# Cross attention in a decoder layer: orders of their own for the second group of heads

## The reference, cut to what matters

```
q = split_heads(x @ Wq)          # x (8, 224, 512), 16 heads of 64
k = split_heads(context @ Wk)    # context (8, 750, 384)
v = split_heads(context @ Wv)
sim = einsum('bhid,bhjd->bhij', q, k) * SCALE
attn = softmax(sim)
out = einsum('bhij,bhjd->bhid', attn, v)
x = layernorm(x + (merge(out) @ Wo + bo))
```

## Time and profile before

| | us |
|---|---|
| median of three runs | 1943.18 |
| the profiled execution, its own time | 1947.31 |
| its span, first to last instruction | 1945.7 |
| step of group one, from Y0 to Y0 | 69.39 |
| step of group two, from Y0 to Y0 | 68.76 |
| steps whose order changes | 8 |

### The profile page before, as it was taken

The page is one execution under the profiler, slowest core; times in us unless marked ns, Lnnn a source line. Parts: engine busy times, 40 slices in busy tenths (PEclk is TensorE's granted clock), DMA queues, the critical chain, the costliest instruction groups (busy, mean ns, idle before and its releaser), DMA issues.

```text
span 1945.7 us, 39197 instructions
## 1 busy us (share of the span) xinstructions
PE 1847.2 (95%) x12618; PEld 1514.6 (78%) x12618; DVE 1471.7 (76%) x3326; ACT 1172.2 (60%) x2568; POOL 999.7 (51%) x1065
## 2 busy tenths in 40 slices
PE   5999998999998999999999999999999999988997
PEld 4777776777776898899899888888888888874443
DVE  5677677788888777777777777877777777777887
ACT  5676776675675466566656666655555555554664
POOL 0343443244343266665675644567677667540554
PEclk9899999999997999999999999999999999999999
DMA  4321323011113414322431432313332331252221
GB/s 127 125 71 61 103 80 105 29 38 47 29 46 108 153 46 139 120 93 96 140 99 62 158 104 60 104 49 92 107 87 64 84 107 44 66 125 72 65 65 60
DMA packets 109571, 166.76 MB, mean 86 GB/s; under 512 B 32488, under 2 KB 67672, under 8 KB 109512
## 3 DMA queue, kind: packets, MB, share of 16 engines
q1 hardware_dynamic: 91016, 129.77, 21.7%
q0 software_dynamic: 14656, 28.92, 5.2%
q10 hardware_dynamic: 3840, 7.34, 1.3%
HBM read 109.25 MB, written 50.46 MB: 82 GB/s over the span
## 4 chain that ended last, share of the span: by engine, by line
PE 56%; DVE 16%; issue 11%; ACT 5%; POOL 5%; DMA 5%; POOLq 0%; SPq 0%; DVEq 0%; ACTq 0%
PE att_ps_P L1477 9%; PE att_ps_P L1489 9%; PE att_ps_T L1523 7%; PE att_ps_O L1537 6%; PE att_ps_SA L1512 5%; PE att_ps_O L1548 4%; PE att_ps_P L1466 4%; PE att_ps_T L451 3%; DVE sa_sums L751 2%; PE att_ps_SB L513 2%; DMA out_dram<-ff_y_out 2%; DVE ca_big L1772 2%; DVE att_ps_O L1904 1%; DMA sa_ff_in<-in_L_ffn_w_gate_dram 1%; PE att_ps_P L468 1%
## 5 line engine op out<-in xcount | busy, mean ns | idle before, releaser
L1345 POOL TENSOR_TENSOR ca_pr<-ca_pr,ca_rec 112x750 f32<-112x750 f32 x256 | 364.2, 1440 | 249.6 <-DVE ca_rec L1767 247.0
L392 POOL TENSOR_TENSOR sa_p_lo<-sa_pr,sa_p_hi 112x448 fp32r<-112x448 f32 x128 | 147.9, 1161 | 330.2 <-ACT sa_p_hi L599 330.2
L1657 ACT ACTIVATE ca_big<-att_ps_T 126x448 fp32r<-126x448 f32 x374 | 204.0, 546 | 137.9 <-PE att_ps_T L1523 134.0
L1772 DVE TENSOR_TENSOR ca_big<-att_ps_T,ca_big 126x448 fp32r<-126x448 f32 x374 | 231.8, 620 | 36.3 <-ACT ca_big L1657 28.4
L1489 PE MATMUL att_ps_P<-ca_w_hi,ca_ct 128*126 128x256 f32 x1152 | 236.8, 290 | 4.7 <-DVE ca_v_st L1755 4.2
L1523 PE MATMUL att_ps_T<-att_ident,ca_pr 112*126 112x112 f32 x1496 | 211.9, 263 | 8.0 <-DVE ca_big L1772 6.2
L1477 PE MATMUL att_ps_P<-ca_ct,ca_w_hi 128*128 128x376 f32 x768 | 201.4, 343 | 0.0
L1523 PEld LDWEIGHTS att_ps_T<-att_ident,ca_pr 112*126 112x126 f32 x1496 | 159.6, 140 | 51.7 <-issue 26.6
L1489 PEld LDWEIGHTS att_ps_P<-ca_w_hi,ca_ct 128*126 128x126 f32 x1152 | 185.5, 187 | 15.8 <-issue 8.5
L1537 PE MATMUL att_ps_O<-ca_big,ca_v_st 126*128 126x448 f32 x756 | 183.6, 378 | 5.8 <-DVE ca_big L1772 3.0
L1489 PE MATMUL att_ps_P<-ca_w_lo,ca_ct 128*126 128x256 f32 x576 | 162.3, 282 | 0.0
(11 more groups left out here) (271 smaller groups left out, 5611.8 us busy)
## 6 DMA issues: line engine op xcount, KB each, us to landing
ct_kept<-ca_ct SPq DMA_DIRECT2D x8, 1134.0 KB, 9.1
ca_ct<-ct_kept POOLq DMA_DIRECT2D x8, 1134.0 KB, 7.1
ct_kept<-ca_ct SPq DMA_DIRECT2D x8, 1116.0 KB, 11.4
ca_ct<-ct_kept POOLq DMA_DIRECT2D x8, 1116.0 KB, 10.9
sa_xin<-in_x_dram SPq DMA_DIRECT2D x16, 448.0 KB, 3.7
xt_kept<-ca_xt SPq DMA_DIRECT2D x8, 896.0 KB, 4.9
ca_xt<-xt_kept POOLq DMA_DIRECT2D x8, 896.0 KB, 4.9
ternary<-ca_stage SPq DMA_DIRECT2D x36, 172.0 KB, 1.9
```

The source lines that it names most:

```text
L392: pool.tensor_tensor(p_lo[:, h % NB, :], pr[:, h % NB, :], f32(p_hi[:, h % NB, :]), ALU.subtract).then_inc(p_split, 1)
L1345: pool.tensor_tensor(w, w, rec[:, h % PB, c:c + 1].to_broadcast([R, S]), ALU.mult).then_inc(norm_done, 1)
L1657: act.activation(weights_view(h, t, False), blocks_view(source.bank, t), ACT.Copy).then_inc(t_hi_done, 1)
L1772: dve.tensor_tensor(weights_view(h, t, True), blocks_view(source.bank, t), f32(weights_view(h, t, False)), ALU.subtract).then_inc(source.d ...
```

## The change

The second group gets orders of its own on PE, ACT and DVE, instead of the common order with XT and CT skipped. The list of projection units that says which bank each uses gets a second form as well. The common orders stay as they were for the first group, the orders of POOL and SP too, and no arithmetic changes. The 66 units of PE, 72 of ACT and 105 of DVE in a step are the same ones as before, moved. At the switch between the groups, the splits of new weights that hung on XT0, XT1, CT00, K30, K31, V11 and V13 hang on T3.0, Q0, K31, V11, V12 and V13.

Below, each "-" order is the one before with XT and CT taken out, as it is carried out in the second group; each "+" order is the new one.

```diff
-    UNITS = """XT0 XT1 CT00 Q0 CT01 CT02 CT10 CT11 V00 V01 V02 Q1 Q2 CT12 K00 K01 K10 K11 K20 K21 V03 Q3 V04 V05 V10 K30 K31
-               V11 V12 V13 V14 V15""".split()
+    UNITS_2 = """Q0 V00 V01 V02 Q1 Q2 K00 K01 K10 Q3 K11 K20 K21 V03 V04 V05 K30 V10 K31 V11 V12 V13 V14 V15""".split()
...
# PE
-  S2.1 T3.0 Q0+ T3.1 O2 T3.2 S3.0 T4.0 O3 T4.1 V00+ V01+ T4.2 S3.1 V02+ T5.0 Q1+ Q2+ T5.1 O4 T5.2 K00+ K01+ T6.0 K10+ T6.1
-  K11+ T6.2 O5 S0.0+ T7.0 K20+ K21+ T7.1 O6 V03+ T7.2 S0.1+ Q3+ O7 T0.0+ V04+ V05+ T0.1+ S1.0+ V10+ T0.2+ Y0 S1.1+ T1.0+ Y1
-  T1.1+ K30+ K31+ O0+ S2.0+ T1.2+ V11+ V12+ T2.0+ V13+ V14+ T2.1+ V15+ O1+ T2.2+
+  S2.1 T3.0 Q0+ T3.1 O2 T3.2 S3.0 T4.0 O3 T4.1 V00+ V01+ T4.2 S3.1 V02+ T5.0 O4 Q1+ T5.1 Q2+ T5.2 K00+ T6.0 K01+ T6.1 O5
+  K10+ T6.2 S0.0+ Q3+ T7.0 K11+ K20+ T7.1 O6 K21+ T7.2 S0.1+ V03+ V04+ T0.0+ O7 V05+ S1.0+ T0.1+ K30+ T0.2+ V10+ Y0 S1.1+
+  T1.0+ Y1 T1.1+ K31+ S2.0+ T1.2+ V11+ O0+ T2.0+ V12+ V13+ T2.1+ V14+ O1+ T2.2+ V15+
# ACT (cut)
-  T3.0 S4.1 Q0+ T3.1 S5.1 O2 T3.2 T4.0 S6.0 O3 T4.1 S7.0 V00+ V01+ T4.2 V02+ S6.1 T5.0 S7.1 ...
+  T3.0 S4.1 T3.1 S5.1 O2 Q0+ T3.2 T4.0 O3 S6.0 T4.1 S7.0 V00+ V01+ T4.2 T5.0 V02+ O4 S6.1 ...
# DVE
-  M4.1 T3.0 M5.1 Q0+ T3.1 R4.1 R5.1 O2 T3.2 M6.0 T4.0 ... M2.0+ M3.0+ V10+ R2.0+ T0.2+ R3.0+ Y0 M2.1+ M3.1+ T1.0+ R2.1+ R3.1+
-  Y1 F0 T1.1+ F1 K30+ F2 O0+ F3 K31+ F4 M4.0+ F5 T1.2+ F6 V11+ F7 M5.0+ F8 V12+ F9 R4.0+ F10 T2.0+ F11 V13+ F12 V14+ F13
-  T2.1+ F14 R5.0+ V15+ O1+ T2.2+
+  M4.1 T3.0 M5.1 R4.1 T3.1 O2 T3.2 R5.1 Q0+ M6.0 T4.0 ... M2.0+ K30+ M3.0+ T0.2+ R2.0+ Y0 V10+ M2.1+ M3.1+ T1.0+
+  Y1 F0 T1.1+ F1 R3.0+ F2 F3 F4 K31+ M4.0+ F5 T1.2+ R2.1+ F6 M5.0+ V11+ T2.0+ F7 V12+ O0+ F8 R3.1+ F9 F10 T2.1+ F11 F12
+  V13+ F13 V14+ R4.0+ F14 T2.2+ R5.0+ O1+ V15+
...
-                       B - 1: {"XT0": [7], "XT1": [8], "CT00": [9], "K30": [10], "K31": [11], "V11": [12], "V13": [13]}}
+                       B - 1: {"T3.0": [7, 8], "Q0": [9], "K31": [10], "V11": [11], "V12": [12], "V13": [13]}}
...
+    def order_for(orders, ahead):
+        return orders[ahead.group if ahead else GROUPS - 1]
...
-                    if ahead and not (ahead.group and name[0:2] in CACHED):
+                    if ahead:
```

More of the change, by code:

```diff
@@ L1019, in banks @@
         return Banks(slots)
[L1021 to L1024, removed]
+    assert sorted(UNITS_2) == sorted(u for u in UNITS_1 if u[0:2] not in ("XT", "CT"))
+    UNITS = [UNITS_1, UNITS_2]
+    plans, front = [banks(units) for units in UNITS], banks(FRONT)
+    last_units = UNITS_1[UNITS_1.index("V10"):]
+    assert sorted(FRONT) == sorted(UNITS_1) and FRONT[-len(last_units):] == last_units
     def batch(b, g, ahead=0):
@@ L1549, in project_out @@
             mm.then_inc(to.filled, 1)
-        ORDER = steps("""XT0+ XT1+ S2.1 T3.0 CT00+ Q0+ T3.1 CT01+ O2 T3.2 CT02+ CT10+ S3.0 T4.0 CT11+ O3 T4.1 V00+ V01+ T4.2 S3.1 V02+
+        ORDERS = [steps("""XT0+ XT1+ S2.1 T3.0 CT00+ Q0+ T3.1 CT01+ O2 T3.2 CT02+ CT10+ S3.0 T4.0 CT11+ O3 T4.1 V00+ V01+ T4.2 S3.1 V02+
                    T5.0 Q1+ Q2+ T5.1 O4 CT12+ T5.2 K00+ K01+ T6.0 K10+ T6.1 K11+ T6.2 O5 S0.0+ T7.0 K20+ K21+ T7.1 O6 V03+ T7.2
                    S0.1+ Q3+ O7 T0.0+ V04+ V05+ T0.1+ S1.0+ V10+ T0.2+ Y0 S1.1+ T1.0+ Y1 T1.1+ K30+ K31+ O0+ S2.0+ T1.2+ V11+ V12+
-                   T2.0+ V13+ V14+ T2.1+ V15+ O1+ T2.2+""")
+                   T2.0+ V13+ V14+ T2.1+ V15+ O1+ T2.2+"""),
+                  steps("""S2.1 T3.0 Q0+ T3.1 O2 T3.2 S3.0 T4.0 O3 T4.1 V00+ V01+ T4.2 S3.1 V02+ T5.0 O4 Q1+ T5.1 Q2+ T5.2 K00+
+                           T6.0 K01+ T6.1 O5 K10+ T6.2 S0.0+ Q3+ T7.0 K11+ K20+ T7.1 O6 K21+ T7.2 S0.1+ V03+ V04+ T0.0+ O7 V05+
+                           S1.0+ T0.1+ K30+ T0.2+ V10+ Y0 S1.1+ T1.0+ Y1 T1.1+ K31+ S2.0+ T1.2+ V11+ O0+ T2.0+ V12+ V13+ T2.1+
+                           V14+ O1+ T2.2+ V15+""")]
         def do(name, at, place=in_loop):
-            if name in UNITS:
+            if name in UNITS_1:
                 unit(name, at)
@@ L1685, in step @@
             splits = split_at(g, b)
-            for name, next_batch in ORDER:
+            for name, next_batch in order_for(ORDERS, ahead):
                 if name in splits:
@@ L1832, in vector @@
                    M2.0+ M3.0+ V10+ R2.0+ T0.2+ R3.0+ Y0 M2.1+ M3.1+ T1.0+ R2.1+ R3.1+ Y1 F0 T1.1+ F1 K30+ F2 O0+ F3 K31+ F4 M4.0+ F5 T1.2+
-                   F6 V11+ F7 M5.0+ F8 V12+ F9 R4.0+ F10 T2.0+ F11 V13+ F12 V14+ F13 T2.1+ F14 R5.0+ V15+ O1+ T2.2+""")
+                   F6 V11+ F7 M5.0+ F8 V12+ F9 R4.0+ F10 T2.0+ F11 V13+ F12 V14+ F13 T2.1+ F14 R5.0+ V15+ O1+ T2.2+"""),
+                  steps("""M4.1 T3.0 M5.1 R4.1 T3.1 O2 T3.2 R5.1 Q0+ M6.0 T4.0 M7.0 O3 T4.1 R6.0 V00+ T4.2 V01+ R7.0 M6.1 T5.0
+                           O4 V02+ Q1+ T5.1 Q2+ T5.2 R6.1 M7.1 T6.0 K00+ T6.1 K01+ O5 K10+ T6.2 R7.1 M0.0+ Q3+ M1.0+ R0.0+ T7.0
+                           K11+ K20+ T7.1 O6 K21+ R1.0+ T7.2 M0.1+ M1.1+ V03+ R0.1+ R1.1+ V04+ T0.0+ V05+ O7 T0.1+ M2.0+ K30+
+                           M3.0+ T0.2+ R2.0+ Y0 V10+ M2.1+ M3.1+ T1.0+ Y1 F0 T1.1+ F1 R3.0+ F2 F3 F4 K31+ M4.0+ F5 T1.2+ R2.1+
+                           F6 M5.0+ V11+ T2.0+ F7 V12+ O0+ F8 R3.1+ F9 F10 T2.1+ F11 F12 V13+ F13 V14+ R4.0+ F14 T2.2+ R5.0+ O1+
+                           V15+""")]
         def do(name, at, g=None, b=None, place=in_loop):
-            if name in UNITS:
+            if name in UNITS_1:
                 lo_of(name, at)
```

23 lines of the change are left out of this document (15 added, 8 removed).

## The result

The changed kernel takes 1959.55 us (median of 4 runs, 1957.70 to 1961.36), the kernel before 1943.26 beside it (4 runs, 1940.18 to 1943.39). The ratio is 1.0088, 95% interval 1.0070 to 1.0105: slower, by 16 us between the medians. The profiled executions stand at 1947.31 and 1959.89, 12.6 apart. The forecast was +12 from one to the other and 1954 for the median.

The account below looks back on a forecast made before the run. PE's work and its waits for banks were taken to bound the kernel. New places -5 us and three holds +17 gave +12: 1959.0 for the profiled execution, 1955 for the median, taken as 1954; range 1937 to 1960.

Parts of the forecast that it names:

- the three holds: DVE links second behind R3.0, R3.1 and R4.0 wait for POOL's normalisation: 0.87 + 0.5 + 1.0 us in seven steps, +17.
- the first: R3.0 before F2, F3, F4: F3 held by N3.0, T2.0 waits 0.87 us on PE, bounds 0 and about 1.1.
- the third: R4.0 before F14: second scaling held by N4.0, T3.0 +0.6 us, T3.1 another 0.4, +1.0 in all, bounds 0 and 1.4.
- The second: R3.1 before F9, F10: F10 held by N3.1, T2.2 and V15 late on PE, +0.5 us, bounds 0 and 0.9.
- What the new places take away: PE's bank waits in group two: V15 -0.52 us, T3.0 -0.3, changes of kind -0.1, in all -0.9 a step.
- T4.0's 0.2 for the copy of Q0: ACT copies Q0 before T3.2, so T3.2's copy comes 0.2 us later and T4.0 waits for it on PE: +0.2.
- T5.2's wait of 0.2: On PE between T5.1 and T5.2, Q2 replaces O4; the wait of 0.2 us was to stay.
- the changes of kind: Changes of kind between neighbours on PE, about as many as before: -0.1 us a step.
- The late context: KC is issued behind N5.0 on POOL, so V00 gets the kept context late: up to 0.2 us a step, put at nothing.
- The holds without the integer link: Rival: F3 and F4 pass beside N3.0, the other two holds bite; +6 us, 1949; chance 0.2.
- The rival by which the gains stand: Holds fall into DVE's free time or scalings miss N4.0; holds under 0.7 us a step; -5 us, 1938; chance 0.27.
- The rival by which FT2 holds as well: FT2, queued behind N3.0 on POOL, holds F4 (+11 us, 1965) or only F5 (1957); chance 0.11.

Follow-up runs that it names:

- r_as_before: r3_r4_kc with R2.1 and R3.1 also back ahead of Y1, as in the kernel before: 1950.36 us, 1.0029 to the kernel before.
- scalar_normalise: The changed kernel with POOL's normalisation as a tensor_scalar, one semaphore increment ahead of it, not a tensor_tensor: 1977.95 us, 1.0164 to the kernel before.
- r4_behind_f14: The changed kernel with R4.0 behind F14 on DVE, not ahead of it: 1958.21 us, 1.0067 to the kernel before.
- r3_r4_kc: The changed kernel with R3.0 back ahead of Y0, R4.0 behind F14 and KC ahead of N5.0: 1946.77 us, 1.0010 to the kernel before.
- before_r4_behind_f11: The kernel before with R4.0 behind F11 on DVE, not ahead of F10: 1942.76 us, 0.9978 to the kernel before.
- before_scalar_normalise: The kernel before with POOL's normalisation as a tensor_scalar, not a tensor_tensor: 1962.05 us, 1.0079 to the kernel before.

## Why the prediction was right or wrong

**What bounds the kernel, and the three holds.** Right, each at its place in six of six steps, and F3, the one that no row of before showed, among them. Undone by themselves, the first took away 0.77 (forecast 0.87) and the third 1.12 (0.62 at T3.0 and 0.50 at T3.1; forecast 1.0). The second was only undone together with other edits (r_as_before, scalar_normalise); V15's wait went in both. It measured 0.25 where 0.5 was forecast: T2.2, which stands before V15 on PE, is late by less than 0.1, so only V15 pays.

**What the new places take away.** V15's 0.52 and T3.0's 0.31 went as said, where no hold is in the way (V15 0.00 in r_as_before, T3.0 0.00 in r4_behind_f14). T4.0's 0.2 for the copy of Q0 measured 0.17 and went when the copy was moved. Two small terms were wrong. T5.2's wait of 0.2 did not stay, it went, and Q2 got one of 0.10. And the changes of kind cost instead of gaining: a step less its waits is 66.6 to 66.8 before, by how the smallest distances are counted, and 0.1 to 0.2 more in r3_r4_kc, where -0.1 stood. Less V15's 0.25, r3_r4_kc would come to about 68.3 without holds, 0.5 below before where 0.6 was forecast. That is an estimate from its steps; the run that was to show it, r_as_before, caught F3 instead.

**The rest at nothing.** The late context was given 0 to 0.2 a step; it took 0.15 to 0.31 in five steps and 0.83 in one, 0.32 in the mean. And it is more than a term: what a repair wins ahead of V00 can land in it until KC is issued earlier (r4_behind_f14: 0.9 of 1.12). FT2, N7.1 and what is queued behind them cost Y0 nothing.

**The sum.** A step of 70.4 was forecast, 70.83 in the mean measured; +12 and 1959.0 for the profiled execution, +12.6 and 1959.89 measured. That this is so near is in part luck. The parts whose order changed cost 13.8 and not 12: the context (0.32 a step, put at nothing), the changes of kind and the third hold were sized too low, the second hold, the first and T5.2 too high, and low outweighed high by 0.3 a step. Against that, 1.5 us fell away at the end of the kernel, where nothing was changed. The gain of 0.9 in the step of the switch, for 0.6, is another thing than the prediction has: it says that holds can happen only where the links do, and the kernel before had one there (the split of 1.62).

**The step that failed** is the move to the median. I took 4.1 us off, the distance of before's profiled execution from its median, as if the changed kernel's would lie as high; it lies 0.3 above its own. And I took another 1 off because the holds were laid out with cover "at its smallest", which the traces did not bear out. Without both, the same sum forecasts 1959 for a measured 1959.55. With both it forecasts 1954, 11 above before, and 16 was measured; by the ratio, 1.0088 times the 1943.18 before is 1960.3, past the 1960 at which the range ends. Part of the 4.1 can be seen. From the output projection of the last batch to the end, before's execution takes 189.7, the changed kernel's and before_r4_behind_f11's 188.1. Among the thirteen kernels but before's, ten take 187.7 to 188.7 there and three 189.9 to 190.0, and nothing in that part differs. So about 1.5 us of the 4.1 can have belonged to that execution and not to the kernel. The other 2.6 stay open.

**The rivals.** The holds without the integer link fell with the first row of F3. The rival by which the gains stand fell too: no hold cost PE nothing, and the three (2.1 us a step) are well above the 0.7 at which it would have decided. The rival by which FT2 holds as well fell at F5, which takes 0.15 at 1303.34 while FT2 runs to 1303.89. So the rule of the Trainium skill, "SBUF — State Buffer", section "Who interferes with whom", on DVE instructions with two SBUF inputs, does not hold for the whole length of a POOL TENSOR_SCALAR. Nor is this form without effect: beside the TENSOR_SCALAR product, F4 and F11 were held for its first 0.9 us, and F3 in before_scalar_normalise for its last 0.6. The prediction read from L1819 beside L1373 that this form does not hold at all; L1819 starts 0.60 after L1373 when most of those 0.9 had passed, and could hardly show it.

## What to carry to other kernels

When a small instruction lets another engine start a large one, what stands second behind it on the first engine can be held for as long as the large one runs. Put such a trigger behind the whole chain of small dependent steps, or where a long gap follows: one place further only moves the hold to the next link, as F12 showed. Look at when the other engine will run and not only where the trigger stands. A wait that is repaired is worth only the distance to the next one in line: undo it together with that one before judging it. And set a sum made on one execution against the fixed parts of a second execution before moving it to a median by the distance of the first.

## What the runs showed of the hardware

- An int32 TENSOR_SCALAR of 112x2 on DVE, 0.17 by itself, takes 1.35 when it starts 0.11 after a TENSOR_TENSOR of 112x750 on POOL, and ends with it; an f32 one of the same shape that starts 0.09 before it takes 0.17.
- The same product as a TENSOR_SCALAR takes 2.18 for 1.44. A link that starts in its first 0.4 us is free 0.90 to 0.93 after its start (F4 0.74, F11 0.50). An int32 TENSOR_SCALAR of 112x2 that starts 1.59 after it is held to its end (F3 0.59 for 0.15), a TENSOR_TENSOR of 112x2 that starts 1.67 after it is not (0.14).
- A SCALAR_TENSOR_TENSOR of 128x512 on DVE, 0.68 by itself, takes 1.62 when it starts 0.36 after the two-input product.
- A product on POOL beside the two scalings of 112x512 takes 1.66 for 1.44: POOL pays too.
- Two halves of a transfer (1134 and 1116 KB over 8 issues) landed after 7.0 and 10.7 us where a write of another queue was issued 1.5 us ahead, after 10.2 and 13.9 where it was issued 0.4 us behind the first half, and after 7.6 and 12.0 where it was 0.7 us behind. The write took 3.1 us in the first case and 3.9 to 4.1 in the others.
